# Fewer stalls around the pipeline's start and the hidden layer's bound: instructions reordered and three of them moved to other engines

## The chip, the cores and the metric

The kernel runs on one core of a Trainium2 chip. The metric is the device time of one execution in microseconds (us); lower is better. A core has five engines that run their own instruction streams in order and meet only at semaphores: PE (TensorE, matrix multiplications), DVE (VectorE), ACT (ScalarE), POOL (GpSimd) and SP (SyncE, which here issues most DMA transfers). A reader who wants to know why an instruction started when it did asks two things: what stood ahead of it on its own engine, and which semaphore it waited for.

## The reference

One transformer layer with both norms after their sums, T = 4096 tokens, D = 256, 16 heads of 16, a window of 128 keys, and a hidden layer of 1024:

```
q = l2norm(x @ Wq.T); k = l2norm(x @ Wk.T); v = x @ Wv.T          # per head
attn = softmax(q k^T - slope_h * |i - j|, over keys j with 0 <= i - j < ... 128)
x = layernorm(x + concat_heads(attn v) @ Wo.T)
bw1 = mean|w1| per row * sign(w1);  bw2 = mean|w2| per row * sign(w2)
h = gelu(x @ bw1.T + b1);  x = layernorm(x + h @ bw2.T + b2)
```

## The kernel before

The attention runs over 32 blocks of 128 tokens. Each block needs the keys of its own block and of the one beside it. A "step" i computes the scores of block i in four chunks of four heads, and does beside it other blocks' work, so that the engines overlap:

- PE, in this order: scores of chunks 0 and 1 (L398, `scores`), queries and keys of block i+3 (L431, `project_qk`), the output projection of block i-4 (L451), the values of block i+1 (L442, `project_v`), scores of chunks 2 and 3, and the weighted sum of the values of block i-2 (L421, `weighted_sum`, four chunks). A chunk's scores wait until the exponentials two chunks before have emptied their bank; the first waits for the transposed queries and keys of its block as well. The first half of a weighted sum waits for the first pair of tiles that POOL cuts in step i-1, the second half for the second pair (`cut_ready`).
- ACT: four exponentials (L706), one per chunk, and between them the 16-bit high halves of the normalised queries and keys of block i+2 (L673, L676), the squares of block i+3 (L659), the logarithm and exponential of their norm (L664, L666) and a copy that doubles block i+2's low halves (L686).
- POOL: the low halves of block i+2 (L1367, L1372), and for each pair of chunks the two tiles of the window's mask, its own block's and its neighbour's (L1349).
- DVE: the transposition, reciprocal, scaling and second transposition of a weighted sum (L881 to L897), a rounding step of the norm (L870 to L874), the normalised rows (L976), the sum to the residual and its statistics (L911 to L922), the sums of squares (L953), the values times a fading factor (L945), and the seed of the norm (L865).
- SP: a transposing DMA (L284, `turn_parts`) that turns a block's parts into `qkT`, and two loads for a later block (L271, L272, `load_block`).

The order inside a step is written by hand; nothing plans it. The first four steps and what stands ahead of them (the "head") are written out apart, since nothing is there yet to overlap with. In it PE runs passes on constants (`keep_warm`, L493): 8 at the start, 14 ahead of the first scores and 6 behind step 1 (each gives two records in the profile). Block 4's queries and keys and the later ones go into PSUM banks 0 and 2, the values into bank 1, scores into banks 3 to 6, weighted sums and output projections into bank 7.

Towards the attention's end the hidden layer is prepared. Its intermediate is scaled by a bound that is taken from the row sums of |w1| (`abs_w1`, L1043) and the biases' sizes (`size_of_bias`, L1106). Three instructions of DVE (`bound_rows`) add them (L1112), take the largest of each partition (L1114) and scale the row sums (L1115). They stand ahead of the weighted sum of block 26 being turned (`turn_sums`, L881). The rest of the time, from about 230 us, is the hidden layer (L552) and the second layer (L577).

## Time and profile before

| | us |
|---|---|
| median of 3 runs | 350.33 (350.27 to 350.53) |
| the profiled execution | 350.25 |
| its span, first to last instruction | 348.5 |
| PE busy | 331.0 (95%) |
| ACT busy | 293.9 (84%) |
| DVE busy | 287.0 (82%) |
| POOL busy | 270.1 (77%) |

The profiled execution takes 1.75 us more than its span, for what lies before the first and behind the last instruction. It stands 0.08 us below the median of the runs. All later rows come from this one execution. PE is busy for 95% of the span, but this is an average: between 160 and 200 us it does not stop at all, while there are gaps in the first 45 us and again between 205 and 225 us.

### The profile page before, as it was taken

The page shows a single profiled execution, that of the slowest core. Times are in us where ns is not written, and L with a number is a line of the kernel's source. Part 1 is how long each engine was busy: PE and PEld are TensorE (multiplying, and loading weights), DVE is VectorE, ACT ScalarE, POOL GpSimd, SP SyncE. Part 2 cuts the span into 40 slices and gives each one's busy share as a digit, 9 for nine tenths or more (in the row PEclk, how much of TensorE's full clock was granted, in tenths as well). Part 3 has the DMA queues.
Part 4 walks back from the last instruction along what each step waited for, and adds up shares of the span by engine and source line. Part 5 has one row for each costly group of instructions (what it writes and reads, how often), then busy time and mean ns, then how long its engine had stood idle before and what let it go on. Part 6 is the DMA issues. An engine that isn't in the chain of part 4 may idle for free.

```text
span 348.5 us, 12141 instructions
## 1 busy us (share of the span) xinstructions
PE 331.0 (95%) x4269; PEld 226.6 (65%) x4269; DVE 287.0 (82%) x751; ACT 293.9 (84%) x495; POOL 270.1 (77%) x322
## 2 busy tenths in 40 slices
PE   8798998999999999999999988899999999999991
PEld 6555676667667667677677666566666666666681
DVE  5875889789998987887889997688879899888674
ACT  2689988889989989989989969889788888897752
POOL 1149998978989999989999968795597885765342
PEclk9999999999999999999999999999999999999997
DMA  7577955565466465676687753020221240521113
GB/s 234 128 126 184 193 125 108 103 133 127 92 134 136 99 142 122 149 168 163 158 164 182 151 98 62 4 62 2 60 62 62 63 120 2 121 83 38 60 62 121
DMA packets 99493, 38.35 MB, mean 110 GB/s; under 512 B 84736, under 2 KB 98432, under 8 KB 99328
## 3 DMA queue, kind: packets, MB, share of 16 engines
q1 hardware_dynamic: 99456, 37.89, 47.9%
q8 instruction: 19, 0.31, 0.4%
q14 instruction: 18, 0.15, 0.1%
HBM read 12.72 MB, written 4.19 MB: 49 GB/s over the span
## 4 chain that ended last, share of the span: by engine, by line
PE 85%; DVE 6%; ACT 3%; issue 3%; DMA 1%; DVEq 0%; POOLq 0%; POOL 0%; SPq 0%
PE ps L552 16%; PE ps L577 16%; PE ps L421 15%; PE ps L431 15%; PE ps L398 8%; PE ps L442 7%; PE ps L451 6%; ACT prob L706 2%; DMA qkT<-parts 1%; PE ps L461 1%; PE ps L493 1%; PE ps L500 1%; DVE ss L953 1%; DVE faded L945 1%; ACT sq L659 1%
## 5 line engine op out<-in xcount | busy, mean ns | idle before, releaser
L1349 POOL TENSOR_SCALAR_AFFINE_SELECT prob<-prob 128x1024 f32<-128x1024 f32 x126 | 133.9, 1099 | 2.3 <-ACT prob L706 2.2
L706 ACT ACTIVATE prob<-ps 128x1024 f32<-128x1024 f32 (+1 forms) x128 | 121.8, 1004 | 11.8 <-PE ps L398 11.4
L421 PE MATMUL ps<-prob,faded 128*17 128x128 f32 x2016 | 61.4, 273 | 1.2 <-issue 1.2
L431 PE MATMUL ps<-wqkv,xt 128*128 128x512 f32 x124 | 61.4, 617 | 1.1 <-DVE qkn L976 1.1
L552 PE MATMUL ps<-yT,sgn 128*128 128x512 f16 x256 | 60.8, 379 | 0.0
L780 ACT ACTIVATE ps<-ps,bias,alpha 128x512 f32<-128x512 f32 x64 | 47.6, 751 | 14.6 <-PE ps L552 12.0
L421 PEld LDWEIGHTS ps<-prob,faded 128*17 128x17 f32 x2016 | 52.2, 97 | 7.8 <-issue 4.9
L1420 POOL TENSOR_TENSOR resid<-z,resid 128x256 f32 (+1 forms) x31 | 22.5, 728 | 26.8 <-DVE z L1185 26.8
L398 PE MATMUL ps<-qkT 64*64 64x192 f16 (+3 forms) x1024 | 36.1, 254 | 5.8 <-ACT prob L706 2.4
L552 PEld LDWEIGHTS ps<-yT,sgn 128*128 128x128 f16 x256 | 24.8, 98 | 23.9 <-issue 0.2
L398 PEld LDWEIGHTS ps<-qkT 64*64 64x64 f16 x1024 | 20.9, 105 | 25.7 <-issue 25.6
L1367 POOL TENSOR_TENSOR parts<-qkn,parts 128x256 f16<-128x256 f32 x30 | 20.4, 680 | 20.4 <-ACT parts L676 20.3
L431 PEld LDWEIGHTS ps<-wqkv,xt 128*128 128x128 f32 x124 | 21.1, 189 | 21.2 <-issue 18.1
L1372 POOL TENSOR_TENSOR parts<-qkn,parts 128x512 f16<-128x512 f32 x29 | 34.4, 1185 | 0.0
L442 PE MATMUL ps<-wqkv,xt 128*128 128x256 f32 x128 | 33.4, 383 | 0.4 <-DVE otok L890 0.4
L881 DVE STREAM_TRANSPOSE turned<-ps 128x512 f32<-128x512 f32 x32 | 22.9, 715 | 11.5 <-PE ps L421 10.4
L577 PE MATMUL ps<-sgn,w 128*128 128x256 f16 x256 | 30.6, 273 | 0.0
L451 PEld LDWEIGHTS ps<-wo,oT 128*128 128x128 f32 x112 | 21.1, 190 | 13.9 <-issue 12.2
L577 PEld LDWEIGHTS ps<-sgn,w 128*128 128x128 f16 x256 | 25.0, 98 | 6.3
L451 PE MATMUL ps<-wo,oT 128*128 128x256 f32 x112 | 29.0, 381 | 0.0
L577 PE MATMUL ps<-sgn,prob 128*128 128x256 f16 x240 | 28.3, 273 | 0.0
L442 PEld LDWEIGHTS ps<-wqkv,xt 128*128 128x128 f32 x128 | 23.5, 190 | 5.8 <-issue 2.3
(110 smaller groups left out, 558.2 us busy)
## 6 DMA issues: line engine op xcount, KB each, us to landing
xt<-in_xT SPq DMA_DIRECT2D x32, 128.0 KB, 2.2
resid<-in_x SPq DMA_DIRECT2D x32, 128.0 KB, 2.3
out_dram<-resid SPq DMA_DIRECT2D x7, 512.0 KB, 2.9
w<-in_w2T SPq DMA_DIRECT2D x1, 1024.0 KB, 7.0
w<-in_w1T SPq DMA_DIRECT2D x4, 256.0 KB, 3.2
w_nat<-in_w SPq DMA_DIRECT2D x4, 256.0 KB, 3.9
wqkv<-in_wqkvT SPq DMA_DIRECT2D x3, 256.0 KB, 3.9
qkT<-parts SPq DMA_TRANSPOSE x32, 4.3
```

The lines of the kernel that those rows point to most:

```text
L398: mm = nc.tensor.matmul(ps[keys, SC + 2 * (c % 2) + hp, 2 * P * t + first:2 * P * t + last], qkT[row, H // 2 + 2 * c + t, slot, keys], moving,
L421: mm = nc.tensor.matmul(ps[32 * m:32 * m + HD + 1, OT, P * c:P * c + P], v, p, start=(n == 0), stop=(n == 1 or not near))
L431: mm = nc.tensor.matmul(ps[:, QK[slot % 2], :], xt[:, slot, k, :], wqkv[:, k, 0:2 * D], start=(k == 0), stop=(k == DC - 1))
L442: mm = nc.tensor.matmul(ps[:, VO, 0:D], xt[:, slot, k, :], wqkv[:, k, 2 * D:3 * D], start=(k == 0), stop=(k == DC - 1))
L451: mm = nc.tensor.matmul(ps[:, OT, D * par:D * par + D], oT[:, par, k, :], wo[:, k, :], start=(k == 0), stop=(k == DC - 1))
L552: mm = nc.tensor.matmul(ps[:, bank, :], sgn1[:, c, P * k:P * k + P], yT[:, par, a, c, :, :], start=(m == 0), stop=(m == 2 * DC - 1))
L577: mm = nc.tensor.matmul(ps[:, banks[b], 0:D], hid[par][:, a, k, P * b:P * b + P], sgn2[:, k, :], start=(m == 0), stop=(m == 2 * HC - 1))
L706: nc.scalar.activation(to, scored, ACT.Exp, scale=QK_SCALE ** -2).then_inc(exp_done, 1)
L780: nc.scalar.activation(bank, bank, ACT.Gelu, bias=bias1[:, k:k + 1], scale=alpha1[:, k:k + 1]).then_inc(gelu_done, 1)
L881: nc.vector.transpose(turned[:].rearrange("p b d -> p (b d)"), ps[:, OT, :]).then_inc(sums_turned, 1)
L1349: return nc.gpsimd.affine_select(out=at, in_=at, compare_op=ALU.is_ge, fill=0.0, base=-near, pattern=[[0, 2 * CH], [1 if near else -1, P]] ...
L1372: nc.gpsimd.tensor_tensor(parts[:, par, H:2 * H, 2:4, :], src[:, H:2 * H, :].unsqueeze(2).to_broadcast([P, H, 2, HD]), parts[:, par, H:2 * ...
```

## The change

Two places are changed. The first is the head. PE projects the queries and keys of block 3 and the values of block 1 ahead of the first scores, the later projections move one block forward each, and the constant passes fall from 14 and 6 to 6 and 0. The values of the first five blocks get places of their own (`first_values`: bank 1, the two halves of bank 7 and so on), so that the projections need not wait for DVE. In step 3 the last two chunks of scores stand behind the weighted sum of block 1. ACT makes the high halves of block i+3, not i+2, behind the third exponential; in step 3 it has only the four exponentials. POOL makes low halves of block i+3 between the two pairs of cuts in steps 0 to 2 and none in step 3. DVE takes over three doubling copies from ACT, and splits a sum of |w2| in two. Two of the first transfers are issued by ACT, and SP's transpositions and loads change their order. The second place is the bound: POOL does the addition and the scaling behind the cuts of step 28, and DVE only takes the largest, later.

```diff
@@ the constants, the banks of the first values
-WARM_AGAIN = 14
-WARM_BETWEEN = 6
+WARM_AGAIN = 6
+HEAD = 3
+EARLY = 5
+first_values = (ps[:, VO, 0:D],) + tuple(ps[:, OT, D * half:D * half + D] for half in (0, 1, 0)) + (ps[:, VO, 0:D],)
-            return next3 and (not isinstance(i, int) or i >= 0)
+            return next3 and (not isinstance(i, int) or i > -HEAD)
@@ SP
-            for n in range(DC):
-                sp.dma_start(wqkv[:, n, 0:2 * D], wqkvT[:, n, 0:2 * D]).then_inc(wqk_in[n], 16)
-                sp.dma_start(xt[:, n], xT[n]).then_inc(x_in[n], 16)
-            for n in range(DC, XS):
+            sp.dma_start(wqkv[:, 0, 0:2 * D], wqkvT[:, 0, 0:2 * D]).then_inc(wqk_in[0], 16)
+            for n in range(1, XS):
                 sp.dma_start(xt[:, n], xT[n]).then_inc(x_in[n], 16)
...
-            load_block(XS, 0)
-            turn_parts(0, 0)
-            turn_parts(1, 1)
-            turn_parts(2, 2)
-            load_block(XS + 1, 1)
-            load_block(XS + 2, 2)
-            turn_parts(3, 3)
+            for n in range(2):
+                load_block(XS + n, n)
+                turn_parts(n, n)
+            for n in range(2, XS):
+                turn_parts(n, n)
+                load_block(XS + n, n)
+            turn_parts(XS, 0)
             sp.dma_start(wo[:], woT).then_inc(wo_in, 16)
-            load_block(XS + 3, 3)
...
@@ PE
+            def first_value(n):
+
+                count(pe, v_ready, n if n >= HEAD else 0)
+                pe.wait_ge(x_in[n % XS], (n - n % XS) * (32 // XS) + 16)
+                for k in range(DC):
+                    mm = nc.tensor.matmul(first_values[n], xt[:, n % XS, k, :], wqkv[:, k, 2 * D:3 * D],
+                                          start=(k == 0), stop=(k == DC - 1))
+                mm.then_inc(v_done, 1)
...
-            project_v(0, 0)
+            first_value(0)
             project_qk(2, 2)
-            pe.wait_ge(id_made, 2)
+            pe.wait_ge(consts, 1)
+            first_value(1)
+            project_qk(3, 3)
             pe.wait_ge(consts, 2)
             keep_warm(WARM_AGAIN, SC)
-            step(0, 0, out=False, pv=False, both=False, early=True)
-            step(1, 1, out=False, pv=False, behind=lambda: keep_warm(WARM_BETWEEN, OT))
-            step(2, 2, out=False, early=True)
-            step(3, 3, out=False, early=True)
+            for c in range(2):
+                scores(0, c, 0, 0, False)
+            project_qk(4, 0)
+            for c in range(2, NC):
+                scores(0, c, 0, 0, False)
+            first_value(2)
+            scores(1, 0, 1, 1, True)
+            project_qk(5, 1)
+            for c in range(1, NC):
+                scores(1, c, 1, 1, True)
+            project_qk(6, 2)
+            scores(2, 0, 0, 2, True)
+            first_value(3)
+            scores(2, 1, 0, 2, True)
+            pe.wait_ge(newton, norm_base(2, True) + NORM_OPS)
+            first_value(4)
+            for c in range(2, NC):
+                scores(2, c, 0, 2, True)
+            for c in range(NC):
+                weighted_sum(0, c, 0)
+            for c in range(2):
+                scores(3, c, 1, 3, True)
+            for c in range(NC):
+                weighted_sum(1, c, 1)
+            for c in range(2, NC):
+                scores(3, c, 1, 3, True)
             pe.wait_ge(wo_in, 16)
@@ ACT
+            act.dma_start(xt[:, 0], xT[0]).then_inc(x_in[0], 16)
+            act.dma_start(wqkv[:, 1, 0:2 * D], wqkvT[:, 1, 0:2 * D]).then_inc(wqk_in[1], 16)
...
-            step(0, 0, ln=False, both=False, high_first=True, doubled=False)
-            step(1, 1, ln=False, squares_first=True)
-            step(2, 2, ln=False, squares_first=True)
-            step(3, 3, ln=False, squares_first=True)
+            high_halves(2, 0, first=True)
+            norm_of(0, True, False)
+            for i in range(3):
+                for c in (0, 1):
+                    exps(i, c, i, i > 0)
+                squares(i + 4, i % 2)
+                exps(i, 2, i, i > 0)
+                high_halves(i + 3, 1 - i % 2)
+                exps(i, 3, i, i > 0)
+                if i == 0:
+                    act.wait_ge(v_ready, 1)
+                norm_of(i + 1, True, False)
+            for c in range(NC):
+                exps(3, c, 3)
@@ DVE
             round_of(1, True, False)
             normalise_rows(4, 0)
-            abs_w2(P, P + P // 2)
+            double(3, 1)
...
-            def bound_rows():
-
-                dve.wait_ge(abs_done, 5)
-                nc.vector.tensor_tensor(bound[:], abs_bias[:], alpha1[:], ALU.add).then_inc(abs_done, 1)
-                dve.wait_ge(abs_done, 6)
+            def largest_row():
+
+                dve.wait_ge(bound_summed, 1)
                 nc.vector.tensor_reduce(bound1[:], bound[:], AX.X, ALU.max).then_inc(bound_done, 1)
-                nc.vector.tensor_scalar(alpha1[:], alpha1[:], 1.0 / (D * Y_SCALE), None, ALU.mult).then_inc(abs_done, 1)
...
             size_of_bias()
-            bound_rows()
             turn_sums(NB - 6)
...
             scale_sums(NB - 5, 1)
+            largest_row()
             add_output(NB - 6, 0)
@@ POOL
-            step(0, 0, both=False, low_at=0)
-            step(1, 1, low_at=0)
-            for n in range(2, 5):
-                step(n, n % XS, low_at=0)
+            step(0, 0, both=False, ahead=1)
+            step(1, 1, ahead=1)
+            step(2, 2, ahead=1)
+            step(3, 3, next2=False)
+            step(4, 0, low_at=0)
...
+            def bound_rows():
+
+                pool.wait_ge(abs_done, 5)
+                nc.gpsimd.tensor_tensor(bound[:], abs_bias[:], alpha1[:], ALU.add).then_inc(bound_summed, 1)
+                nc.gpsimd.tensor_scalar(alpha1[:], alpha1[:], 1.0 / (D * Y_SCALE), 1.0, ALU.mult,
+                                        ALU.mult).then_inc(alpha_scaled, 1)
...
-            step(NB - 4, 0, low_at=0)
+            step(NB - 4, 0, low_at=0, behind=bound_rows)
```

On PE, steps 2 and 3 of the head read as follows before (64x192 are scores, 128x512 queries and keys, 128x256 values, 17x128 a weighted sum; steps 2 and 3 have the same five rows each):

```order
L398 MATMUL ps<-qkT 64x192 x16
L431 MATMUL ps<-wqkv,xt 128x512 x2
L398 MATMUL ps<-qkT 64x192 x16
L442 MATMUL ps<-wqkv,xt 128x256 x2
L421 MATMUL ps<-prob,faded 17x128 x32
```

In the changed kernel the same two steps, from the projection ahead of step 2, are:

```order
L428 MATMUL ps<-wqkv,xt 128x512 x2
L395 MATMUL ps<-qkT 64x192 x8
L437 MATMUL ps<-wqkv,xt 128x256 x2
L395 MATMUL ps<-qkT 64x192 x8
L437 MATMUL ps<-wqkv,xt 128x256 x2
L395 MATMUL ps<-qkT 64x192 x16
L418 MATMUL ps<-prob,faded 17x128 x32
L395 MATMUL ps<-qkT 64x192 x16
L418 MATMUL ps<-prob,faded 17x128 x32
L395 MATMUL ps<-qkT 64x192 x16
```

One pair of projections has gone from these steps to earlier ones, and the last sixteen score passes, those of step 3's chunks 2 and 3, stand behind the second weighted sum.

POOL's first steps before (128x1024 are cuts of the mask; 128x16x16 and 128x16x32 the low halves of one block):

```order
L1386 TENSOR_TENSOR parts<-qkn,parts 128x16x16 x2
L1367 TENSOR_TENSOR parts<-qkn,parts 128x16x16
L1372 TENSOR_TENSOR parts<-qkn,parts 128x16x32
L1349 AFFINE_SELECT prob<-prob 128x1024 x2
L1367 TENSOR_TENSOR parts<-qkn,parts 128x16x16
L1372 TENSOR_TENSOR parts<-qkn,parts 128x16x32
L1349 AFFINE_SELECT prob<-prob 128x1024 x4
```

and in the changed kernel:

```order
L1433 TENSOR_TENSOR parts<-qkn,parts 128x16x16 x3
L1394 AFFINE_SELECT prob<-prob 128x1024
L1412 TENSOR_TENSOR parts<-qkn,parts 128x16x16
L1417 TENSOR_TENSOR parts<-qkn,parts 128x16x32
L1394 AFFINE_SELECT prob<-prob 128x1024 x3
L1412 TENSOR_TENSOR parts<-qkn,parts 128x16x16
L1417 TENSOR_TENSOR parts<-qkn,parts 128x16x32
L1394 AFFINE_SELECT prob<-prob 128x1024 x4
L1412 TENSOR_TENSOR parts<-qkn,parts 128x16x16
L1417 TENSOR_TENSOR parts<-qkn,parts 128x16x32
L1394 AFFINE_SELECT prob<-prob 128x1024 x6
```

The low halves now stand between a step's pairs, not ahead of them, and one block of them is missing from step 3, so that six cuts stand together.

DVE around the bound before (the last row turns the weighted sum of block 26):

```order
L1043 TENSOR_REDUCE alpha<-w_nat 128x2
L1106 SCALAR_TENSOR_TENSOR abs_bias<-bias 128x8
L1112 TENSOR_TENSOR bound<-abs_bias,alpha 128x8
L1114 TENSOR_REDUCE bound<-bound 128x1
L1115 TENSOR_SCALAR alpha<-alpha 128x8
L881 STREAM_TRANSPOSE turned<-ps 128x512
```

and in the changed kernel, the place itself and the later one:

```order
L1082 TENSOR_REDUCE alpha<-w_nat 128x2
L1154 SCALAR_TENSOR_TENSOR abs_bias<-bias 128x8
L919 STREAM_TRANSPOSE turned<-ps 128x512
L925 RECIPROCAL ps<-turned 128x16
...
L935 STREAM_TRANSPOSE oT<-otok 128x256
L1160 TENSOR_REDUCE bound<-bound 128x1
L949 TENSOR_TENSOR resid<-resid,ps 128x256
```

Two instructions of 8 elements a partition have left DVE, and the third stands one step later.

## Rows read from the trace of the kernel before

**Rows 1.** The page, chain of work that ended last, shares of the span.

```profile
PE 85%; DVE 6%; ACT 3%; issue 3%; DMA 1%; DVEq 0%; POOLq 0%; POOL 0%; SPq 0%
```

**Rows 2.** Windows: us, busy (x) of PE, PEld, DVE, ACT, POOL; clock, DMA, GB/s.

```profile
15.00:20.00 5.00, 3.60 (x46) 2.09 (x44) 4.82 (x9) 3.69 (x10) 1.77 (x3) 1.00 0.96 179
160.00:200.00 40.00, 40.00 (x653) 27.66 (x652) 34.46 (x91) 37.63 (x65) 39.75 (x42) 1.00 0.75 163
```

**Rows 3.** Weight loads, 4 to 8 us: start us, us, what, idle before <-releaser.

```profile
5.67 0.29 PEld L500 LDWEIGHTS ps<-wqkv,xt 128*128 128x128 f32 x1 [0.62 <-DMA wqkv<-in_wqkvT]
6.32 0.19 PEld L500 LDWEIGHTS ps<-wqkv,xt 128*128 128x128 f32 x1 [0.36 <-issue]
```

**Rows 4.** Timeline of PE, 0 to 42 us.

```profile
1.13 3.78 PE L493 MATMUL ps<-mean_ones 128*128 128x128 f32 x16 [1.13 <-DVE mean_ones L1006]
...
12.78 3.29 PE L493 MATMUL ps<-mean_ones 128*128 128x128 f32 x28
17.47 0.42 PE L398 MATMUL ps<-qkT 64*64 64x64 f16 x16 [1.40 <-DMA qkT<-parts]
17.82 1.98 PE L431 MATMUL ps<-wqkv,xt 128*128 128x512 f32 x4
19.73 0.42 PE L398 MATMUL ps<-qkT 64*64 64x64 f16 x16
20.08 1.13 PE L442 MATMUL ps<-wqkv,xt 128*128 128x256 f32 x4
...
40.34 1.98 PE L431 MATMUL ps<-wqkv,xt 128*128 128x512 f32 x4
```

**Rows 5.** Timeline of DVE, 13 to 14 us.

```profile
13.46 0.69 DVE L976 TENSOR_TENSOR qkn<-ps,rnorm 128x512 f32<-128x512 f32 x1
```

**Rows 6.** The transposing DMAs (L284) issued in 0 to 60 us, eight of them.

```profile
DMA to landing us min/median/max: 4.2/4.4/6.0
```

**Rows 7.** Timeline of ACT, 28 to 38 us.

```profile
28.51 1.92 ACT L706 ACTIVATE prob<-ps 128x1024 f32<-128x1024 f32 x2
30.32 0.60 ACT L659 ACTIVATE sq<-ps 128x512 f32<-128x512 f32 x1
30.80 0.42 ACT L673 ACTIVATE parts<-qkn 128x256 f16<-128x256 f32 x1
...
31.62 1.95 ACT L706 ACTIVATE prob<-ps 128x1024 f32<-128x1024 f32 x2
```

**Rows 8.** Timeline of POOL, 32 to 38 us.

```profile
32.00 0.67 POOL L1367 TENSOR_TENSOR parts<-qkn,parts 128x256 f16<-128x256 f32 x1
...
33.75 4.23 POOL L1349 TENSOR_SCALAR_AFFINE_SELECT prob<-prob 128x1024 f32<-128x1024 f32 x4
```

**Rows 9.** Timeline of DVE, 203 to 206.5 us.

```profile
203.66 0.16 DVE L1106 SCALAR_TENSOR_TENSOR abs_bias<-bias 128x8 f32<-128x8 f32 x1
203.85 0.94 DVE L1112 TENSOR_TENSOR bound<-abs_bias,alpha 128x8 f32<-128x8 f32 x1
204.83 0.16 DVE L1114 TENSOR_REDUCE bound<-bound 128x1 f32<-128x8 f32 x1
204.91 0.94 DVE L1115 TENSOR_SCALAR alpha<-alpha 128x8 f32<-128x8 f32 x1
205.76 0.70 DVE L881 STREAM_TRANSPOSE turned<-ps 128x512 f32<-128x512 f32 x1
```

**Rows 10.** Timeline of PE, 203 to 212 us.

```profile
203.83 0.52 PE L398 MATMUL ps<-qkT 64*64 64x192 f16 x16
...
206.57 1.07 PE L421 MATMUL ps<-prob,faded 128*17 128x128 f32 x32 [1.25 <-issue]
...
211.59 0.36 PE L398 MATMUL ps<-qkT 64*64 64x192 f16 x8 [0.57 <-ACT prob L706]
```

**Rows 11.** Timelines of ACT and of POOL, 205 to 211 us.

```profile
209.07 0.42 ACT L673 ACTIVATE parts<-qkn 128x256 f16<-128x256 f32 x1 [2.58 <-DVE qkn L976]
210.16 0.68 POOL L1367 TENSOR_TENSOR parts<-qkn,parts 128x256 f16<-128x256 f32 x1 [3.29 <-ACT parts L676]
```

More of the change, by code:

```diff
@@ L280, in turn_parts @@
                 count(sp, s_done, scored)
[L281 to L282 removed]
+                if isinstance(n, int) and (n < HEAD or n == NB - 1):
+                    sp.wait_ge(first_low, n + 1 if n < HEAD else HEAD + 1)
                 sp.wait_ge(parts_ready, doubled)
@@ L687, in double @@
                                      ACT.Copy).then_inc(parts_ready, 1)
-            def step(i, slot, next2=True, next3=True, ln=True, both=True, norm=True, high_first=False,
-                     squares_first=False, doubled=True, before_rows=None, amid=None, tail=None):
-                par = slot % 2
-                own, near = OWN_AT[slot], NEAR_AT[par]
-                at = slice(near, own + 1, own - near)
-                def exps(c):
-                    act.wait_ge(s_done, i * NC + c + 1)
-                    if c == 0:
-                        count(act, pv_done, i - 2)
-                    banks = ps[:, SC + 2 * (c % 2):SC + 2 * (c % 2) + 2, :]
-                    if both:
-                        to = prob[:, at, CH * c:CH * c + CH, :].rearrange("p s h q -> p h s q")
-                        scored = banks.rearrange("p b (t s q) -> p (b t) s q", t=2, s=2)
-                    else:
-                        to = prob[:, own, CH * c:CH * c + CH, :]
-                        scored = banks.rearrange("p b (t q) -> p (b t) q", t=2)[:, :, P:2 * P]
-                    nc.scalar.activation(to, scored, ACT.Exp, scale=QK_SCALE ** -2).then_inc(exp_done, 1)
-                if high_first:
-                    high_halves(i + 2, par)
-                exps(0)
-                exps(1)
-                if next2 and not high_first and not squares_first:
@@ new lines, in exps @@
+            def exps(i, c, slot, both=True):
+                own, near = OWN_AT[slot], NEAR_AT[slot % 2]
+                at = slice(near, own + 1, own - near)
+                act.wait_ge(s_done, i * NC + c + 1)
+                if c == 0:
+                    count(act, pv_done, i - 2)
+                banks = ps[:, SC + 2 * (c % 2):SC + 2 * (c % 2) + 2, :]
+                if both:
+                    to = prob[:, at, CH * c:CH * c + CH, :].rearrange("p s h q -> p h s q")
+                    scored = banks.rearrange("p b (t s q) -> p (b t) s q", t=2, s=2)
+                else:
+                    to = prob[:, own, CH * c:CH * c + CH, :]
+                    scored = banks.rearrange("p b (t q) -> p (b t) q", t=2)[:, :, P:2 * P]
+                nc.scalar.activation(to, scored, ACT.Exp, scale=QK_SCALE ** -2).then_inc(exp_done, 1)
@@ L713, in step @@
+            def step(i, slot, next2=True, next3=True, ln=True, doubled=True, before_rows=None, amid=None, tail=None):
+                par = slot % 2
+                exps(i, 0, slot)
+                exps(i, 1, slot)
+                if next2:
                     high_halves(i + 2, par)
```

82 lines of the change are left out of this document (45 added, 37 removed).

## The prediction

> **What bounds the kernel now.** I read the page first, its chain of waits: PE makes up 85% of the chain that ended last, DVE 6%, ACT 3% and waits for issue another 3% [rows 1]. So a gain has to shorten PE's work or one of PE's waits. The windows come second. They say where such waits are: in the steady stretch from 160 to 200 us PE is busy for all of its 40.00 us, and POOL for 39.75 of them, while between 15 and 20 us PE works for 3.60 of 5.00 us [rows 2]. Two things are to be seen there. PE loses time only at the pipeline's ends, which is where the change is; and POOL is so nearly full that it can't be given much inside the steady stretch. Third comes PE's timeline of the start, where PE's work and its gaps can be walked through instruction by instruction [rows 4], with those of ACT and POOL beside it [rows 7, 8]. Last come the timelines around the bound, where DVE is late and three engines stand idle one after the other [rows 9 to 11].
>
> **The bound, on DVE.** The addition and the scaling, 8 elements a partition, take 0.94 us each [rows 9]. The transposition of block 26's weighted sum stands behind them and starts at 205.76 without a gap, so it is late because of them. The weighted sum itself was done before 203.83, where PE starts the scores that stand behind it [rows 10], and the sizes of the biases are done at 203.66 + 0.16 = 203.82 [rows 9]. In the changed kernel the transposition follows these directly, at about 203.9, that is 205.76 - 203.9 = 1.8 us earlier. What hangs on it:
> - PE's next weighted sum starts at 206.57 after 1.25 us of idle time, so PE was free at 205.32 [rows 10]. The turned sums would be there at 203.9 + 0.7 = 204.6, and the wait goes: -1.25 on PE.
> - DVE then makes the last block's normalised rows 1.8 us earlier. ACT's high halves wait for them until 209.07, after 2.58 us of idle time [rows 11]; they come 1.8 us earlier, at 207.3, and the exponentials behind them too.
> - PE's scores at 211.59 wait 0.57 us for such an exponential [rows 10]. PE was 1.25 us ahead already, the exponential is 1.8 us ahead, so the scores start at the later of 211.59 - 0.57 - 1.25 = 209.8 and 211.59 - 1.8 = 209.8.
>
> So this part is worth 1.25 us for certain if the wait is what it looks like, and 1.8 us if nothing else comes in. I take -1.7, since what follows is a little of both. The bounds are 0 (below) and -2.0.
>
> What it adds: two instructions on POOL behind the cuts of step 28. POOL is idle for 3.29 us before it starts its low halves at 210.16 [rows 11]. The trace shows no such small instruction of this form on POOL, so its cost is bounded by rows: 0.16 us, the sizes of the biases on DVE, from below and 0.94 from above [rows 9]. POOL's cuts end when they did, and what it waits for comes 1.8 us earlier, so 3.29 - 1.8 = 1.49 are left as cover. At 0.94 each the two would cost 1.88 - 1.49 = 0.4, at 0.16 each nothing; I take nothing, since DVE's 0.94 were taken beside POOL's cuts, which are over by then. The largest of each partition (0.16 [rows 9]) stays on DVE one step later and can hold the sum to the residual by 0.16 at most; PE doesn't wait for that one. It waits for POOL's addition, and POOL's cuts of that step have ended long before.
>
> Why the two took 0.94 while the sizes of the biases, 8 elements as well, took 0.16, is open: both stand beside POOL's cuts. The Trainium skill, "GPSIMD Engine Reference", section 1 (specifications), says that GpSimd shares its SBUF interfaces with VectorE, with contention for VectorE's instructions in a two-port mode or with two SBUF inputs. The addition at 203.85 fits that, but the one at 203.66 takes its operand from SBUF twice, ran beside the same cuts and took 0.16 [rows 9], and the scaling has one input and took 0.94. By the rule alone only the addition would leave with a gain, about 0.8; by the rows both do. The sum goes by the rows.
>
> **The start.** Four edits act before the first scores.
> - The first loads are issued earlier, two of them by ACT. The weights of the third pass of the first projection were released by a DMA at 5.67, but the next load ran at 6.32 behind the pass before it, without a DMA in its way [rows 3]. PE's passes were the limit then. I take 0 (bounds -0.4 and +0.4, the latter if ACT's issue of two transfers delays its table).
> - Block 3's queries and keys (1.91 us: 17.82 to 19.73) and block 1's values (about 1.06) move ahead of the first scores [rows 4]. That is 2.97 us of PE's work out of the part behind 17.4 us. They need room ahead of it. The bank for block 3 is free when block 1's normalised rows are done, at 13.46 + 0.69 = 14.15 at the latest [rows 5]; the projection ends at 16.0.
> - The constant passes fall from 28 records to 12. One takes 3.29 / 28 = 0.1175 us [rows 4], so they take 1.41, and end at 17.4.
> - The first transposition lands about 17.1 to 17.5, as before: PE waited for it from 16.07 to 17.47 [rows 4]. The two meet, and the first scores start at 17.4 (before: 17.47). Nothing is won there yet.
>
> **From the first scores to step 4.** From 17.4: chunks 0 and 1 of step 0, 0.35; block 4's queries and keys, 1.91; chunks 2 and 3, 0.35; block 2's values, 1.06: 21.07. One chunk of step 1, 0.25, then block 5's queries and keys, 1.91, then chunk 1 with about 0.4 until ACT sees it: 23.7 [rows 4]. An exponential takes 0.91 in a row of them and 1.0 alone [rows 7]. So step 1's second exponential ends at 24.7 to 24.9; I take 24.8.
>
> From there POOL is what limits. Four cuts take 4.20 us (33.75 to 37.95, the end less the overlap), a pair 2.10; one block's low halves take 33.75 - 32.00 = 1.75 [rows 8]. Between 24.8 and the end of step 2's cuts stand four pairs and two blocks of low halves: 8.4 + 3.5 = 11.9. Is POOL ever held by ACT's high halves? Those of block 4 are ready at 24.8 + 0.48 (squares) + 0.91 (exponential) + 0.82 (high halves) = 27.0, and POOL wants them at 24.8 + 2.1 = 26.9 [rows 7, 8]. Just in time, so no. The cuts of step 2 end at 36.7, where they ended at 33.75 + 4.23 = 38.0 before: 1.3 earlier.
>
> And yet PE gets nothing from it, because of one added wait. The second half of block 1's weighted sum waits for step 2's last cuts, and the scores of step 3's chunks 2 and 3 now stand behind it. PE starts that half at 36.7; a half takes 1.07 with its tail [rows 10], about 1.0 until the next may start: 37.7. Scores and hand-over, 0.4: 38.1. Then two exponentials, 0.91 + 1.0: 40.0. ACT has nothing to do in between but these, since its only work in step 3 is the four exponentials. The second chunk of step 4 needs the last of these (a bank), and block 7's projection stands behind it: 40.0 + 0.3 + 0.3 = 40.6. Before, this projection started at 40.34 [rows 4]. The head gains nothing and loses 0.3. From step 4 on both programs have the same work for PE, which is the bound there [rows 2]; this 0.3 is carried to the end.
>
> Bounds of this: -0.1 (every hand-over 0.1 shorter) to +0.8. The doublings that DVE takes over and the split sums of |w2| lie beside PE's and POOL's work; DVE is 4.82 of 5.00 us busy between 15 and 20 us [rows 2], so this is where they would come out, at 0.3 each and no more.
>
> **Sum.** Against the profiled execution of 350.25 (its span 348.5 and 1.75 around it): -1.7 and +0.3 give 348.85. The median of the runs is 0.08 above that execution, so I predict **348.9 us**. The forecast's own range is 348.2 to 349.8.
>
> **The rivals.**
> - B, a late transposition. Eight transpositions landed between 4.2 and 6.0 us after issue, median 4.4 [rows 6]. Block 1's is issued some 2 us after its normalised rows, at about 16.2 [rows 5], and PE wants it at 21.07. Landing after 4.4 it is there at 20.6, after 6.0 at 22.2, which is 1.1 late, and everything behind it, POOL's chain above all, is late by as much. 348.9 + 1.1 = 350.0. For it speaks that DMA is busy for 0.96 of 15 to 20 us [rows 2] and that two loads now stand between the transpositions on SP's queue; against it, that seven of eight took less.
> - C, POOL as the bound after the head. POOL's cuts of step 4 start at 33.75 + 2 x (4.20 + 1.75) = 45.65 before. In the changed kernel the high halves of block 6 come at 40.0 + 1.9 + 0.82 = 42.7, the low ones at 44.5: 1.15 earlier [rows 7, 8]. If POOL, 39.75 of 40.00 us busy [rows 2], carries the steady stretch and PE's full 40.00 only look like it, the head gives -1.15, not +0.3: 348.9 - 1.45 = 347.5. Against it speaks the chain, with no share of POOL's to speak of [rows 1].
> - E, the bound brings nothing: the stall before 206.57 is marked as issue, not as DVE [rows 10], so it could have another cause. Then 350.25 + 0.3 + 0.08 = 350.6. Against it, the turned sums at 205.76 + 0.70 = 206.46 and the start at 206.57 fit too well.
> - D, on the other side: the clock. PE has new idle time: some 2 us up to 36.7, with the first half of the weighted sum done, and again most of 38.1 to 40.0, with only about 1.4 us of work (1.0 and 0.4) between; 14 constant passes are gone too. If TensorE's clock fell from 2.4 to 1.2 GHz in it, passes would take twice as long: the first sixteen records took 3.78 / 16 = 0.236 us each, the later ones 0.1175 [rows 4]. The slow passes lasted from 1.13 to 6.32 at most [rows 3, 4], 5.2 us, of which half is lost: +2.6, so 351.5. It decides only if a gap of 2 us with little about it is enough; before, a gap of 1.40 was followed by a granted clock of 1.00 [rows 2, 4]. The Trainium skill, "TensorE: Matmul & The Clock Gate", section "HAM oscillation", describes kernels that fall back to the slow clock in every gap of this kind; no trace here shows one.
>
> **How the numbers follow.** The forecast gets 0.55, B 0.15, E 0.12, D 0.10, C 0.08. The time predicted is the forecast's. A measurement of this kernel can't tell less than 0.2% from no change: 0.7 us, from 349.6 to 351.0. Faster is nine tenths of the forecast (0.50), all of C (0.08) and a fifth of B (0.03): 0.61. Slower is D (0.10) and 0.03 for B together with a POOL hold of 0.4 and DVE's lateness: 0.13. The rest, 0.26, is no change. The range for 8 in 10 leaves out D and small tails of C and B on either side: 347.5 to 350.8.
>
> **What would show it right or wrong.** The first scores start at 17.4, block 7's projection at 40.6; a start before 40.2 or behind 41.0 proves the head's sum wrong. POOL should run from 24.8 to 36.7 without a gap, and PE should stand idle before the second half of the weighted sum until 36.7. ACT should be idle for about 2.5 us before 38.1. On DVE the transposition should start 1.8 us earlier relative to the work around it, PE's stall of 1.25 should be gone, POOL's two instructions should fall into its idle time. The granted clock should be 1.00 at 34 to 45 us. The prediction is wrong if the distance between the last scores of the head and the attention's end changes by anything but -1.7.

## The result and the profile after: slower, by TensorE's clock

The changed kernel takes 352.80 us in the median of 20 executions (348.46 to 355.74), the kernel before 350.16 in 20 (349.79 to 350.86). The comparison leaves out the seven of the changed kernel's runs that took over 1.5% more than its fastest; with the thirteen left the ratio is 1.0032, with a 95% interval of 1.0017 to 1.0047. That is +0.3%, and +0.75% by the medians of all runs, so the smaller figure lacks the longest executions. 348.9 was forecast. The spread is part of the result: before, 20 runs lie within 1.1 us, now within 7.3, and by and large the longer an execution is, the lower is its mean granted clock: 0.994 at 348.46, 0.986 at 352.58, 0.976 at 355.74. The mean has to be read with care: once PE has finished, the granted clock falls in every profile, at no cost, so a run without any other fall has less than 1 too (0.994 in the profile of the kernel before, 0.992 to 0.997 in its other runs). The profiled execution of the changed kernel took 354.09 (span 352.4, clock 0.978), one of the long ones; it shows the mechanism at full size, and no difference below rests on its total alone.

First the windows of the changed kernel. The columns are, as in [rows 2], the busy time and instructions of PE, PEld, DVE, ACT and POOL, the granted clock, the share of the DMA engines and GB/s:

```profile
20.00:25.00 5.00, 4.08 (x40) 1.91 (x40) 4.58 (x11) 4.71 (x11) 3.84 (x5) 1.00 0.78 159
25.00:30.00 5.00, 3.97 (x20) 1.36 (x13) 1.84 (x3) 3.08 (x7) 4.89 (x6) 0.66 0.57 106
30.00:35.00 5.00, 3.94 (x76) 2.82 (x76) 3.68 (x9) 3.63 (x5) 3.05 (x3) 1.00 0.17 52
35.00:40.00 5.00, 2.70 (x87) 1.87 (x80) 4.20 (x10) 3.81 (x7) 4.09 (x5) 0.96 1.24 202
40.00:45.00 5.00, 3.83 (x65) 2.07 (x57) 4.63 (x8) 2.73 (x3) 2.59 (x3) 0.50 0.97 225
45.00:50.00 5.00, 5.00 (x8) 2.67 (x9) 0.00 (x0) 2.57 (x5) 4.35 (x6) 0.51 0.02 3
```

The granted clock is 0.50, the level of 1.2 GHz, in two stretches. By windows of 1 us the first lasts from 26.0 to 29.4 us; 20 to 25 us had 4.08 us of PE's work, and a further wait followed. The second lasts from 39.6 to 49.9; 35 to 40 us had 2.70 us of work. In its last 5 us PE starts only eight instructions. From 50 to 340 us the clock is 1.00.

PE's timeline of the same stretch (start us, us, instruction, idle before it; dots stand for rows left out, here and below):

```profile
17.31 0.42 PE L395 MATMUL ps<-qkT 64*64 64x64 f16 x16
...
24.76 0.36 PE L395 MATMUL ps<-qkT 64*64 64x192 f16 x8 [0.92 <-ACT prob L733]
26.16 3.58 PE L428 MATMUL ps<-wqkv,xt 128*128 128x512 f32 x4 [1.03 <-DMA resid<-in_x]
...
32.44 1.13 PE L437 MATMUL ps<-wqkv,xt 128*128 128x256 f32 x4 [1.06 <-DVE rnorm L912]
...
39.84 1.91 PE L418 MATMUL ps<-prob,faded 128*17 128x128 f32 x32 [1.67 <-POOL prob L1394]
...
43.44 0.64 PE L395 MATMUL ps<-qkT 64*64 64x256 f16 x8 [0.90 <-ACT prob L733]
...
44.92 3.78 PE L428 MATMUL ps<-wqkv,xt 128*128 128x512 f32 x4
```

A projection of queries and keys takes 1.98 in [rows 4] and 3.58 and 3.78 here; half a weighted sum 1.91 against 1.07 in [rows 10]. Block 7's projection starts at 44.92, where it started at 40.34 [rows 4]. The first scores start at 17.31, so nothing was lost ahead of them. Where the two waits of 0.92 and 1.03 stand now, the kernel before had passes on constants:

```profile
25.09 1.60 PE L493 MATMUL ps<-mean_ones 128*128 128x128 f32 x12
```

The wait at 26.16 is for block 6's load; SP's timeline shows it issued behind two transpositions:

```profile
15.90 5.12 SPq L285 DMA_TRANSPOSE qkT<-parts  x2
21.08 1.15 SPq L272 DMA_DIRECT2D xt<-in_xT  x1
22.28 0.43 SPq L273 DMA_DIRECT2D resid<-in_x  x1
```

At the attention's end, PE (first fence), then DVE and POOL:

```profile
209.86 0.52 PE L395 MATMUL ps<-qkT 64*64 64x192 f16 x16
210.31 1.04 PE L582 MATMUL ps<-yT,sgn 128*128 128x512 f16 x4
211.28 1.07 PE L418 MATMUL ps<-prob,faded 128*17 128x128 f32 x32
...
216.15 0.36 PE L395 MATMUL ps<-qkT 64*64 64x192 f16 x8 [0.43 <-DMA qkT<-parts]
```

```profile
209.70 0.16 DVE L1154 SCALAR_TENSOR_TENSOR abs_bias<-bias 128x8 f32<-128x8 f32 x1
210.00 0.72 DVE L919 STREAM_TRANSPOSE turned<-ps 128x512 f32<-128x512 f32 x1
```

```profile
212.88 0.20 POOL L1447 TENSOR_TENSOR bound<-abs_bias,alpha 128x8 f32<-128x8 f32 x1
213.17 0.21 POOL L1448 TENSOR_SCALAR alpha<-alpha 128x8 f32<-128x8 f32 x1
```

The scores that stood at 203.83 [rows 10] stand at 209.86: by then the start costs 6.03 us in this execution. It was more at first. Step 4's values are projected at 50.05 here and at 43.02 before, 7.03 later, and the missing 1.0 comes back in between, where PE waits twice in the kernel before and not at all in the changed kernel's profile:

```profile
60.41 0.55 PE L398 MATMUL ps<-qkT 64*64 64x192 f16 x16 [1.04 <-issue]
...
77.18 1.10 PE L442 MATMUL ps<-wqkv,xt 128*128 128x256 f32 x4 [0.40 <-DVE otok L890]
```

What these two waits are was not tested.

The weighted sum behind the scores was at 206.57 and is at 211.28, 4.71 later, without its wait of 1.25, and the scores of 211.59 are at 216.15, 4.56 later. So the bound gave 1.5 of the six back by 216 us. The two instructions that took 0.94 each on DVE [rows 9] take 0.20 and 0.21 on POOL, in its idle time.

### The profile page after: what moved, and what is told of

Read it like the earlier page. It is cut to its first block, busy times and chain, and to the rows that moved or that the text cites. A ratio compares the mean times of both kernels' runs of the same rounds, so it can differ in the third digit from the quotient of the medians.

```text
span 352.4 us, 12084 instructions
## 1 busy us (share of the span) xinstructions
PE 334.1 (95%) x4241; PEld 225.6 (64%) x4241; DVE 287.6 (82%) x754; ACT 292.6 (83%) x492; POOL 269.6 (77%) x323
## 4 chain that ended last, share of the span: by engine, by line
PE 86%; DVE 5%; DMA 2%; issue 2%; ACT 2%; POOL 1%; SPq 0%; POOLq 0%; DVEq 0%; ACTq 0%
PE ps L418 16%; PE ps L428 16%; PE ps L582 15%; PE ps L607 13%; PE ps L395 8%; PE ps L457 7%; PE ps L448 7%; DMA qkT<-parts 1%; PE ps L467 1%; DMA resid<-in_x 1%; PE ps L499 1%; PE ps L437 1%; DVE parts L972 1%; POOL prob L1394 1%; PE ps L506 1%
## 5 line engine op out<-in xcount | busy, mean ns | idle before, releaser
L428 PE MATMUL ps<-wqkv,xt 128*128 128x512 f32 x124 | 64.7, 647 | 2.5 <-DVE qkn L1015 1.5
L418 PE MATMUL ps<-prob,faded 128*17 128x128 f32 x2016 | 62.5, 276 | 1.7 <-POOL prob L1394 1.7
L395 PE MATMUL ps<-qkT 64*64 64x192 f16 (+3 forms) x1024 | 37.6, 258 | 3.5 <-ACT prob L733 3.0
L428 PEld LDWEIGHTS ps<-wqkv,xt 128*128 128x128 f32 x124 | 22.1, 197 | 24.3 <-issue 20.2
L1417 POOL TENSOR_TENSOR parts<-qkn,parts 128x512 f16<-128x512 f32 x28 | 33.1, 1180 | 0.0
L607 PEld LDWEIGHTS ps<-sgn,w 128*128 128x128 f16 x256 | 25.1, 98 | 6.3
L448 PE MATMUL ps<-wqkv,xt 128*128 128x256 f32 x108 | 27.9, 381 | 0.0
L607 PEld LDWEIGHTS ps<-sgn,prob 128*128 128x128 f16 x240 | 23.4, 98 | 5.4
```

What stands on the lines that cost most here:

```text
L395: mm = nc.tensor.matmul(ps[keys, SC + 2 * (c % 2) + hp, 2 * P * t + first:2 * P * t + last], qkT[row, H // 2 + 2 * c + t, slot, keys], moving,
L418: mm = nc.tensor.matmul(ps[32 * m:32 * m + HD + 1, OT, P * c:P * c + P], v, p, start=(n == 0), stop=(n == 1 or not near))
L428: mm = nc.tensor.matmul(ps[:, QK[slot % 2], :], xt[:, slot, k, :], wqkv[:, k, 0:2 * D], start=(k == 0), stop=(k == DC - 1))
L448: mm = nc.tensor.matmul(ps[:, VO, 0:D], xt[:, slot, k, :], wqkv[:, k, 2 * D:3 * D], start=(k == 0), stop=(k == DC - 1))
L607: mm = nc.tensor.matmul(ps[:, banks[b], 0:D], hid[par][:, a, k, P * b:P * b + P], sgn2[:, k, :], start=(m == 0), stop=(m == 2 * HC - 1))
L1417: nc.gpsimd.tensor_tensor(parts[:, par, H:2 * H, 2:4, :], src[:, H:2 * H, :].unsqueeze(2).to_broadcast([P, H, 2, HD]), parts[:, par, H:2 * ...
```

## The experiments

Two theories stood against each other. C: PE's gaps at the start let TensorE's clock fall, and the falls are the loss. O: the order itself costs, by its waits. (C is here what the prediction calls rival D; its own rival C, POOL, is another.) Medians are over all runs of a kernel, since it is the clock that spreads them. The ratio is to the kernel before, run beside it. The kernels ran in four groups, and the kernel before took 350.16 beside the changed kernel, 350.18 beside 1 to 4, 350.63 beside 5 to 8 and 350.75 beside 9 and 10 in the median; so medians of different groups can differ by 0.6 us for no reason of the kernel's. Where that matters, the difference to the kernel before is given.

| kernel | runs | median (range), us | ratio (95%) |
|---|---|---|---|
| changed | 20 | 352.80 (348.46 to 355.74) | 1.0032 (1.0017 to 1.0047) |
| 1 bound alone | 11 | 348.54 (347.88 to 349.84) | 0.9956 (0.9941 to 0.9971) |
| 2 start alone | 8 | 354.35 (351.09 to 356.77) | 1.0103 (1.0067 to 1.0139) |
| 3 all gaps filled | 12 | 349.00 (348.13 to 350.13) | 0.9964 (0.9952 to 0.9976) |
| 4 load earlier | 12 | 351.77 (349.98 to 352.88) | 1.0038 (1.0022 to 1.0054) |
| 5 scores between the halves | 11 | 347.61 (346.55 to 350.58) | 0.9925 (0.9899 to 0.9951) |
| 6 as 5, gaps filled | 5 | 347.34 (346.16 to 348.41) | 0.9907 (0.9889 to 0.9925) |
| 7 as 6, load earlier | 5 | 347.62 (346.59 to 349.53) | 0.9917 (0.9890 to 0.9944) |
| 8 as 1, fewer constant passes | 11 | 351.34 (347.78 to 353.65) | 1.0003 (0.9970 to 1.0037) |
| 9 first gaps filled | 6 | 353.29 (352.36 to 354.03) | 1.0085 (1.0069 to 1.0101) |
| 10 long gap filled | 12 | 350.20 (349.37 to 352.84) | 1.0007 (0.9983 to 1.0031) |

**1, the bound alone.** The kernel before, with only this part of the change (in short; its semaphores and the two functions come along):

```diff
-            bound_rows()            # DVE
+            largest_row()           # DVE, behind scale_sums(NB - 5, 1)
-            step(NB - 4, 0, low_at=0)
+            step(NB - 4, 0, low_at=0, behind=bound_rows)
```

> The kernel before with the bound's part alone (two instructions on POOL, the largest of each partition later on DVE). Theory C (the clock): the whole loss of the changed kernel lies in its start, where TensorE's granted clock is 0.50 twice, and the bound's part is worth the 1.7 us forecast: 348.5 us, with a granted clock of 1.00 up to 230 us and no stall of 1.25 before the weighted sum behind the bound. Rival B (the bound): the bound's part costs something, as the changed kernel's new stalls of 0.46 us before two output projections would have it: 350.2 or more.

Measured 348.54, a ratio of 0.9956: -1.5 us, with an interval from -2.1 to -1.0, as forecast. PE's timeline:

```profile
203.74 0.52 PE L398 MATMUL ps<-qkT 64*64 64x192 f16 x16
...
205.16 1.07 PE L421 MATMUL ps<-prob,faded 128*17 128x128 f32 x32
...
209.71 0.36 PE L398 MATMUL ps<-qkT 64*64 64x192 f16 x8
...
212.41 1.10 PE L451 MATMUL ps<-wo,oT 128*128 128x256 f32 x4 [0.46 <-DVE turned L881]
```

Against [rows 10], the first row is 0.09 earlier, the second 1.41 and the third 1.88, so the gain grows between them by 1.8, the number of the forecast. A stall of 0.46 appears later, and doesn't undo it. The rival falls: the bound costs nothing.

**2, the start alone.** The changed kernel without those lines.

> The changed kernel without the bound's part: the new start alone. Theory C (the clock): everything lost is lost here, 352.8 + 1.7 = 354.5 us in the median, with single runs from 350 to 357, since the clock falls for a different time in each. Rival B: the start costs only what the order costs without the clock, +0.3, so 350.5 us.

Measured 354.35: the two parts add up (354.35 - 1.6 = 352.7), and all of the loss is the start's. Its profiled execution is the shortest of the eight, 351.09. In it block 6's load was in time, PE didn't wait for it, and the early fall is missing:

```profile
24.30 0.36 PE L395 MATMUL ps<-qkT 64*64 64x192 f16 x8 [0.93 <-ACT prob L733]
24.59 1.98 PE L428 MATMUL ps<-wqkv,xt 128*128 128x512 f32 x4
...
36.67 1.07 PE L418 MATMUL ps<-prob,faded 128*17 128x128 f32 x32 [1.67 <-POOL prob L1397]
...
40.74 3.78 PE L428 MATMUL ps<-wqkv,xt 128*128 128x512 f32 x4
```

Here the forecast's walk can be compared without a fall ahead of it: the second half of the weighted sum was forecast for 36.7 and starts at 36.67, block 7's projection for 40.6 and starts at 40.74 (with first scores at 16.85, 0.5 earlier than forecast, so the walk is 0.5 short). The clock falls at 38.8 us, in the wait behind the next scores, and is at 0.50 until 45.6, so the projection takes 3.78. The late fall needs no early one.

**3, the gaps filled.** The changed kernel with more work for PE while it waits, in three places, and no wait removed (two are added, for the places that the passes write):

```diff
-            for c in range(1, NC):
+            for c in range(1, NC - 1):
                 scores(1, c, 1, 1, True)
+            pe.wait_ge(v_ready, 3)
+            keep_warm(3, OT)
+            scores(1, NC - 1, 1, 1, True)
+            keep_warm(4, OT)
             project_qk(6, 2)
...
+            pe.wait_ge(exp_done, 2 * NC + 1)
+            keep_warm(4, SC)
             pe.wait_ge(newton, norm_base(2, True) + NORM_OPS)
...
-            for c in range(NC):
+            for c in (0, 1, 0, 1, 0):
+                weighted_sum(1, c, 1)
+            for c in range(2, NC):
                 weighted_sum(1, c, 1)
```

> The changed kernel with PE's waits at the start filled: 3 and 4 passes on constants around the last chunk of step 1, 4 ahead of block 4's values, and the first half of block 1's weighted sum done two and a half times while it waits for the cuts (same results in the same places). No wait is taken away. Theory C: the clock stays at 1.00, so the time is that without the fall, 348.5 to 349.5 us, and single runs lie within 0.5 us. Rival O (the order and the late load): the time is lost in the waits themselves, and filling them gains nothing: 352.8 us or, with passes that run over, 353.3.

Measured 349.00, 12 runs within 2.0 us (more than the 0.5 expected, less than the changed kernel's 7.3). This is the experiment that decides: PE does more, still waits for all that it waited for, and the kernel is 3.8 us faster in the median than the changed one. Theory O says that it gains nothing. The windows:

```profile
25.00:30.00 5.00, 5.00 (x38) 2.92 (x37) 2.40 (x6) 4.23 (x8) 4.89 (x6) 1.00 0.57 106
...
35.00:40.00 5.00, 3.91 (x132) 3.19 (x128) 4.83 (x11) 2.60 (x3) 4.82 (x5) 1.00 0.99 247
40.00:45.00 5.00, 4.18 (x21) 1.95 (x22) 2.53 (x5) 3.80 (x7) 3.25 (x4) 0.71 0.88 134
45.00:50.00 5.00, 5.00 (x105) 3.85 (x105) 2.91 (x8) 3.12 (x6) 3.31 (x4) 0.95 0.20 53
```

The first fall is gone, and of the second a rest stays, from 42.1 to 45.5 us by finer windows, behind the waits of 1.05 and 0.50 ahead of step 4, which weren't filled.

**9 and 10, one filling each.** 9 has the first of the three pieces of that diff, 10 the third.

> The changed kernel with only PE's first gaps filled, 3 and 4 constant passes around the last chunk of step 1 (23 to 26 us). Theory C with two falls of their own: the first fall goes and the second stays. In the changed kernel's profile the first fall lasted 3.3 us and costs half of that, 1.6, the second 9 us and, with PE busy in half of it, about 3: 352.8 - 1.6 = 351.2 us. Theory C1 (the first fall drags the second with it): 349.5 us. Rival N (neither gap alone matters): 352.8 us.

> The changed kernel with only the long gap filled, the first half of block 1's weighted sum done two and a half times while PE waits for POOL's cuts (the same results in the same places). Theory C with two falls: the first stays, the second becomes short: 352.8 - 2.2 = 350.6 us. Theory C1 (the first drags the second): 352 us or more. The sum of what this and the filling of the first gaps win should be the 3.8 us that both together won.

Measured 353.29 for 9, 2.5 above the kernel before beside it, where the changed kernel is 2.6 above: no gain. 350.20 for 10, 0.6 below, so 3.2 of the 3.8. In 9's profile the early fall is gone and the late one is there; all its runs have a mean clock of 0.985 to 0.987, below anything of the kernel before, so each of them very likely has it:

```profile
25.00:30.00 5.00, 5.00 (x38) 3.15 (x38) 2.67 (x5) 4.61 (x9) 5.00 (x6) 1.00 0.57 106
...
40.00:45.00 5.00, 3.67 (x39) 1.65 (x36) 3.79 (x7) 4.58 (x6) 3.22 (x3) 0.62 1.13 178
45.00:50.00 5.00, 5.00 (x39) 3.09 (x41) 1.33 (x4) 1.10 (x3) 3.87 (x4) 0.70 0.09 20
```

In 10's profile the late fall is short, from 42.2 to 45.6 us, and the early one is missing too, though its gap was not filled:

```profile
25.00:30.00 5.00, 3.62 (x24) 1.64 (x24) 2.26 (x5) 4.07 (x8) 5.00 (x6) 1.00 0.57 106
...
40.00:45.00 5.00, 3.94 (x20) 1.66 (x21) 2.77 (x6) 3.98 (x6) 3.07 (x5) 0.72 0.75 138
```

Its runs fall into two groups, eight at 349.37 to 350.50 and four at 352.27 to 352.84 with a lower clock (0.987), as if a second or a longer fall came in some; no trace of the four was kept. So the second fall has a cause of its own, the long gap, and isn't dragged along by the first. It is the larger one. The 351.2 expected of 9 missed by 2, of which the difference between the groups is 0.6. The two gains, 0.1 and 3.2, are 0.5 short of 3.8; the third filling, 4 passes ahead of block 4's values, was not run alone. Why none of 9's six runs is without a fall, while the changed kernel has single runs at 348.5 to 350.0, isn't known.

**4, the load.** `load_block(XS + 2, 2)` ahead of `turn_parts(2, 2)`, and `load_block(XS + 3, 3)` behind `turn_parts(3, 3)`.

> The changed kernel with the load of block 6 issued ahead of block 2's transposition on SP's queue, and block 7's behind block 3's. It takes away the 1.03 us in which PE waited at 25.1 for that load. Theory C, in which any idle time of this kind lets the clock fall: the first fall, which begins at 26 us, goes in most runs, the second at 41 us stays: 350.5 to 351.5 us. Rival O: the load's wait is worth its 1.03 us, 351.8, and the clock does what it did.

Measured 351.77, 1.0 below the changed kernel in the median, but the ratio of the comparison is 1.0038 against 1.0032. Inconclusive. In the profile the load's wait at 25 us and the early fall are gone, while the late fall stays, from 37.8 to 48.1 us. No run of the twelve has a clock above 0.987. With all gaps filled (6 and 7, below) the load's place makes no difference that five runs show, +0.3 with ranges that overlap.

**5, the order of step 3.** The only experiment that shortens the long wait of step 3 rather than covering it:

```diff
-            for c in range(NC):
+            for c in range(2):
                 weighted_sum(1, c, 1)
             for c in range(2, NC):
                 scores(3, c, 1, 3, True)
+            for c in range(2, NC):
+                weighted_sum(1, c, 1)
```

> The changed kernel with step 3's last two chunks of scores between the two halves of block 1's weighted sum, not behind it: the added wait for POOL's cuts no longer stands ahead of the scores. Theory C (the clock falls in PE's gaps, and this was the longest): the second fall, which began near 38 to 41 us in every trace, goes or becomes short; 352.8 - 2 to 3 for the clock and about 1.5 for the scores' order = 348.5 to 349.5 us, with the single runs that have the late load still at 351. Rival O (the order alone): the wait's own price of 1.67 us is won, 351.1 us, and the clock falls as before.

Measured 347.61: 5.2 below the changed kernel in the median (5.7 by the differences to the kernel before), 0.9 under the lower end of what C expected and far from O's 351.1. Why it gained more than C expected isn't shown. PE's timeline and two windows:

```profile
24.36 0.36 PE L395 MATMUL ps<-qkT 64*64 64x192 f16 x8 [0.93 <-ACT prob L735]
25.76 1.98 PE L428 MATMUL ps<-wqkv,xt 128*128 128x512 f32 x4 [1.04 <-DMA resid<-in_x]
...
37.84 1.07 PE L418 MATMUL ps<-prob,faded 128*17 128x128 f32 x32 [0.49 <-POOL prob L1396]
...
39.40 1.98 PE L428 MATMUL ps<-wqkv,xt 128*128 128x512 f32 x4
```

```profile
35.00:40.00 5.00, 3.98 (x106) 2.62 (x99) 4.77 (x11) 4.28 (x6) 5.00 (x6) 1.00 0.83 248
40.00:45.00 5.00, 4.76 (x61) 2.98 (x63) 4.63 (x10) 3.64 (x7) 4.71 (x5) 1.00 0.90 136
```

The wait for the cuts is 0.49 instead of 1.67, the exponentials of step 3 go on, block 7's projection starts at 39.40, 0.9 earlier than in [rows 4], and the clock stays up. The late load is there, with its 1.04, and no fall follows in this execution. Of the 11 runs three lie at 349.2 to 350.6 with a clock of 0.989 to 0.991; the others have 0.993 or more.

**6 and 7, both.** 5 with the first two pieces of the filling; 7 has the load's place of 4 as well.

> The same, with 3 and 4 constant passes around the last chunk of step 1 and 4 ahead of block 4's values. Theory C: no fall is left, 347.5 us, within 0.5 us from run to run, granted clock 1.00 from 20 to 50 us. Rival O: as the run without the constant passes.

> The same again, with block 6's load ahead of block 2's transposition on SP's queue. Theory C: the late load is covered by the constant passes as far as the clock goes, and costs its wait in some runs only; the load's place is worth 0 to 0.5: 347.0 to 347.5 us. Rival L (the late load is the root: it opens the first gap, and the rest follows): it is worth 1 us, as it was without the passes.

Measured 347.34 and 347.62. 6 beats the kernel before by 0.93% (0.75 to 1.11%), and in its profile the clock was 1.00 in every window from 15 to 50 us, as it was in those of 5 and 7. It has the lowest median, though 5 can't be told from it; the runs spread by 2.3 us, more than the 0.5 expected. Rival L finds no support: it wants 1 us from the load's place, five runs of each show +0.3, and the late fall stood in the profiles of 2 and 4 too, where PE didn't wait for the load.

**8, the other direction.** The kernel of experiment 1, with the change's numbers of constant passes only:

```diff
-WARM_AGAIN = 14
-WARM_BETWEEN = 6
+WARM_AGAIN = 6
+WARM_BETWEEN = 0
```

> The kernel before with the bound's part, and with the constant passes cut as in the change: 6, not 14, ahead of the first scores and none behind step 1. Theory C in the form that the passes kept the clock up: PE's gap ahead of the first scores grows from 1.4 to 3.3 us and the one at 25 us from 0.3 to 1.9, the clock falls in some runs, and the time is 349.5 to 352 us. Rival P (the passes were idle decoration, only the change's new waits pull the clock down): 348.5 us as with all of them.

Measured 351.34 against 348.54, with runs from 347.78 to 353.65. Nothing but passes on constants was taken away, and the median is 2.8 us longer, 2.4 by the differences to the kernel before. Rival P falls. The windows and PE's timeline are those of the longest run, 353.65:

```profile
15.00:20.00 5.00, 2.08 (x18) 1.27 (x19) 4.86 (x10) 4.00 (x10) 1.61 (x3) 0.74 0.98 182
20.00:25.00 5.00, 5.00 (x40) 2.23 (x38) 1.61 (x4) 1.57 (x3) 2.88 (x3) 0.58 0.09 17
...
30.00:35.00 5.00, 4.32 (x28) 1.69 (x32) 2.26 (x5) 3.58 (x7) 5.00 (x5) 0.66 0.46 87
```

```profile
17.92 0.64 PE L398 MATMUL ps<-qkT 64*64 64x64 f16 x16 [3.17 <-DMA qkT<-parts]
18.50 3.78 PE L431 MATMUL ps<-wqkv,xt 128*128 128x512 f32 x4
...
30.13 0.36 PE L398 MATMUL ps<-qkT 64*64 64x192 f16 x8 [1.80 <-ACT prob L706]
```

There are two falls, and each stands where passes were taken away: the wait ahead of the first scores is 3.17 instead of 1.40, and the one ahead of step 2's scores 1.80 instead of 0.27. So the experiment changes the passes and with them the waits; it can't tell what fewer passes ahead of a wait of the same length would do.

## Why the prediction was wrong

It failed in the step from rival D to its chance of 0.10, by which the forecast gave the clock a price of nothing. "Before, a gap of 1.40 was followed by a granted clock of 1.00" was taken as evidence that gaps of this size do nothing. The trace could not say so: 28 records of constant passes stood right ahead of that gap [rows 4], and nothing on hand showed it with fewer. The runs show the clock's price in its place: with PE's gaps filled and no wait removed the median is 3.8 us lower (experiment 3), and with passes taken from the old order it is 2.4 to 2.8 higher (experiment 8). The change took passes from two places. Ahead of the first scores a projection of real work came in their stead, and nothing was lost. At 25 us, where 12 records had stood, waits of 0.92 and 1.03 are left, and the early fall comes behind them; with this place filled it is gone from the profile (experiment 9). It is missing as well from the profiles of 5 and 10, where the same waits stand unfilled, so for the early fall alone this is argued and not shown; for the late one the fillings of 3 and 10 and the order of 5 show it. The prediction names the passes for D only in passing, and D's two gaps, before 36.7 and up to 40.0, are those of the late fall alone. With D taken for likely, its 351.5 would have been the forecast; the median is 1.3 above it. D reckoned with one slow stretch of 5.2 us, and the profiled execution has stretches of 3.4 and 10.2.

The Trainium skill, "TensorE: Matmul & The Clock Gate", section "HAM oscillation", tells of a kernel whose every wait for a DMA, of some 3 to 5 us, sets TensorE back to the slow clock. The traces agree that waits do it, and the page speaks for longer ones than the 2 us that D set beside it. They differ in that no single wait here was longer than 1.67 us where the clock fell in the changed kernel, and in that the same waits don't do it in every execution.

The other steps, one by one:
- The bound, -1.7: right. Alone it gives -1.5 (-2.1 to -1.0), by the mechanism told: the wait of 1.25 goes, the rest comes through the exponentials, and POOL's two instructions vanish in its idle time. Their price of 0.16 to 0.94 was bounded rightly, at 0.20 and 0.21. Rival E falls. Of the quoted rule on shared interfaces the prediction tried only the case of two inputs on the scaling, not that of a two-port mode, so "by the rule alone only the addition" doesn't follow; the sum didn't use it.
- The first scores, 17.4: right, 17.31, and in part by luck. With the same code up to there they start between 16.77 and 18.03 in the profiles of experiments 2, 3, 5, 6, 9 and 10, as the first projection of all takes 1.88 us in some and 3.07 in another. Rival B did not take place: the scores of step 1 start without a wait.
- The walk to step 4: right in form. POOL's cuts do hold the weighted sum, and the wait was forecast for the right place and time (36.7 against 36.67 in experiment 2, where a start 0.5 earlier makes up for a walk 0.5 too short). I counted it as harmless because it cost PE only 0.3 against before, and didn't ask what a PE that does 2.70 us of work in 5 does to the clock, though the text for D says exactly that.
- Waits were missed: of 0.92 for an exponential at 24.76, of 1.06 for a norm's rounding step at 32.44, and one for block 6's load, which was issued at 21.08 behind two transpositions, was wanted at 25.1 and came at 26.16. The text names loads between transpositions only for rival B. With the gaps covered the load's place moves nothing that five runs show (6 and 7).
- "This 0.3 is carried to the end": wrong as a rule. In the profiles 7.03 us of loss at 50 us are 6.03 at 210, since PE was not the bound throughout: the kernel before loses 1.44 in two waits there. For the same reason the way from step 4 to the attention's end, which was to change by -1.7 and nothing else, is 7.03 - 4.56 = 2.5 shorter from 50 to 216 us.
- Without a fall the forecast seems to hold: the two runs of the changed kernel with the highest mean clocks, 0.994 and 0.997, took 348.46 and 349.79, around 348.9, and experiment 3, with most of the falls gone, 349.0. None of the first two was traced.
- Rival C, POOL as the bound behind the start, is not supported: it wants 347.5, and both of these runs took longer. Experiment 5 doesn't decide it. There POOL's cuts of step 4 and PE's projection are both early (the projection by 0.9), but PE then waits 0.82 us at 60.01, and at 203.74 it stands exactly where it stands in experiment 1.

## What to carry to other kernels

Passes on constants, and any projection that stands in a wait, can have a price when they are moved or cut: the clock of what follows. When a change makes a gap on TensorE or lengthens one, look at what PE does around it and not at the gap alone, and time the kernel in many executions: a spread that grew from 1 us to 7 was the sign here. Where PE waits for another engine's last piece, let independent work stand ahead of the wait, not behind it: experiment 5, which did so, gained more than any filling.

## What was not expected of the hardware

- The fall is not decided by the program alone. The same kernel ran with mean clocks from 0.976 to 0.997. Two executions with nearly the same waits at 25 us (1.03 after 0.92, and 1.04 after 0.93) went one with a fall (changed kernel) and one without (experiment 5), and the code is the same up to there. What separates them is open.
- The first fall came behind two waits of only 0.92 and 1.03 us, with work between them, and at a wait of 1.40, behind 28 records of passes, the kernel before had none.
- The clock stayed at 0.50 in nearly the whole of 45 to 50 us, in which PE was busy without a pause.
- An 8-element instruction that takes 0.94 us on DVE beside POOL's cuts takes 0.20 on POOL itself, behind them.

On this last point the trace of the kernel before shows more than the prediction read from it. POOL's cuts of that time, from its timelines of 202.7 to 204.6 and 204.8 to 205.7 us:

```profile
202.62 2.16 POOL L1349 TENSOR_SCALAR_AFFINE_SELECT prob<-prob 128x1024 f32<-128x1024 f32 x2
204.73 1.09 POOL L1349 TENSOR_SCALAR_AFFINE_SELECT prob<-prob 128x1024 f32<-128x1024 f32 x1
```

The addition ends at 203.85 + 0.94 = 204.79, the second cut at 204.78; the scaling ends at 204.91 + 0.94 = 205.85, the third cut at 205.82 [rows 9]. Each ends with the cut that was running, as if it had waited for it. That would make the 0.94 the rest of a cut and no cost of the instruction; no run tested it.
